# Linear attention: turning the keys with VectorE's block transposes and sixteen small transfers a block instead of TensorE's transposes

## The chip, the cores and the metric

The kernel runs on one core of a Trainium2 chip. The metric is the device time of one execution in microseconds (us), the median of several runs. TensorE is written PE (its matrix products) and PEld (its weight loads), VectorE DVE, ScalarE ACT, GpSimd POOL, and the queue of SyncE, which issues most transfers, SP. SBUF is the on-chip memory of 128 partitions, PSUM the accumulator that TensorE writes.

## The reference, cut to what matters

A two-layer model on a hidden state of 4 x 1024 tokens x 256. The change is in the second layer's attention: linear attention with 16 heads of dimension 128 and a decay for each head. The kernel works with blocks of 128 tokens (the reference with blocks of 32, which gives the same sums):

```
q, k, v = silu(x @ w_qkv)            # per head
for each block of tokens:
    inter = (q * q_decay) @ kv                   # kv: the head's state, 128 x 128
    intra = ((q @ k.T) * diag_decay) @ v
    kv    = block_decay * kv + (k * k_decay).T @ v
    out   = inter + intra
out = rmsnorm(out) * gate; y = out @ w_out
```

The product `(k * k_decay).T @ v` sums over tokens, so TensorE wants the keys with tokens on the partitions. The projections leave them with the head's dimension on the partitions (`kT`), as `q @ k.T` wants them. So each block of keys is turned, 128 x 128 for each of the four sequences.

## The kernel before, in words

The program is a row of phases; the one in question, `linear_attention_phase`, runs from about 1224 to 2630 us. Its engines run their own instruction lists and meet at semaphores. A loop goes over eight pairs of heads; within a pair, sixteen steps are written out, one for each block c of 128 tokens (0 to 7) and each head j of the pair (0, 1). One step works on all four sequences: tiles are 128 partitions x 4 x 128 columns of float32. A state is needed by the next block only, so keys are turned and states made for blocks 0 to 6: fourteen turns in a pair, 112 in all.

TensorE's order within a step i with c < 7 (lines of the profile in brackets):

1. scores S = k q of this step (L1996, eight products),
2. **four transposes of this step's keys** into the PSUM tile KT (L2003),
3. the projections of the next step's queries and keys into PJ (`project_qk`, L1937),
4. output O = v sd (L2018), and, from block 1, O += kv qd (L2021),
5. the state's product KT = kd v (L2026), into the same PSUM tile KT that held the turned keys,
6. the projections of values (L1968) and of the next step's gate (L1937),
7. the output projection (L1981).

For blocks with c = 7 the transposes and the state's product are missing. In blocks with c = 0 item 4 has half its products.

VectorE's order in a step: `sd` = S times the decays (L2101); `kd` = turned keys times their decay, read from KT (L2107); `go` = gate times O (L2116); `kv`, the state, updated from KT (L2121, L2124); `gol`, the low part of go (L2130); the output sum (L2083, two halves). ScalarE makes `qT` (L1867) and `kT` (L1871) of the next step from PJ, then goh, the squares, the values and the gate. `kT` has two buffers, one for each j; KT, kd and O have one.

SP loads the next pair's decays and weights at the beginning of each pair, once the buffers are free (`load_decays` L1807, `load_pair` L1801 to L1803), and does nothing else in this phase.

Of the kernel before, what the change touches and what calls it, by code (L numbers as in the profile page):

```python
# [21 lines left out]
ALU = mybir.AluOpType  # L22
# [3 lines left out]
P = 128  # L26
# [14 lines left out]
def done(step):  # L41

    return step + 1 + CREDIT
# [35 lines left out]
def give_credit(eng, *sems):  # L79
    for s in sems:  # L80
        eng.sem_inc(s, CREDIT)  # L81
# [1653 lines left out]
def linear_attention_phase(nc, X, XH, XL, ident, raw, wo_raw, dec_in, w_qkv, w_gate, w_out, rms_w, decays, kdec, bdec,  # L1735
# [5 lines left out]
    H, DH, BLK = LH, 128, LBLK  # L1741
    NBLK = SEQ // BLK
    HD = H * DH
    B4 = BATCH
    with Phase(nc, "lin") as ph:
# [10 lines left out]
        kT = ph.sb("kT", [P, 2, B4, BLK])  # L1756
# [2 lines left out]
        qd = ph.sb("qd", [P, B4, BLK])  # L1759
        sd = ph.sb("sd", [P, B4, BLK])  # L1760
        kd = ph.sb("kd", [P, B4, DH])
        kv = ph.sb("kv", [P, 2, B4, DH])
        o2 = ph.sb("o2", [P, B4, BLK])
        go = ph.sb("go", [P, B4, BLK])
# [4 lines left out]
        KT = ph.ps("KT", [P, B4, P])  # L1769
# [1 line left out]
        OUT = ph.ps("OUT", [P, 2, 2, D])  # L1771
        VP = ph.ps("VP", [P, 2, 2 * DH])
        (w_in, wo_in, wo_scaled, woh_ready, act_goh, dve_gol, rms_in, dec_loaded, x_in, dec_ready, wh_ready, wl_ready, wo_ready, memsets, sum_set,
         pe_q, pe_k, pe_v, pe_g, pe_s, pe_kt, pe_o, pe_kv, pe_out0, pe_out1, pe_sum,
         act_q, act_k, act_v, act_g, act_sq, pool_qd, pool_sum,
         dve_sd, dve_kd, dve_kv, dve_go, dve_acc0, dve_acc1, mean_ready, root_ready) = ph.sems(
            "w_in wo_in wo_scaled woh_ready act_goh dve_gol rms_in dec_loaded x_in dec_ready wh_ready wl_ready wo_ready memsets sum_set "
            "pe_q pe_k pe_v pe_g pe_s pe_kt pe_o pe_kv pe_out0 pe_out1 pe_sum "
            "act_q act_k act_v act_g act_sq pool_qd pool_sum "
            "dve_sd dve_kd dve_kv dve_go dve_acc0 dve_acc1 mean_ready root_ready")  # L1780
        pe_out = (pe_out0, pe_out1)
        dve_acc = (dve_acc0, dve_acc1)
        xh = XH[:].rearrange("p k (b c l) -> p k b c l", b=B4, c=NBLK)
        xl = XL[:].rearrange("p k (b c l) -> p k b c l", b=B4, c=NBLK)
        acc_v = acc[:].rearrange("p (b c) n -> p b c n", b=B4)
# [4 lines left out]
        HP, TURNS = H // 2, 2 * NBLK  # L1790
        LAST = NBLK - 1
        STATES = 2 * LAST
        block = ph.block()

        @block.sync
        def _(sp):
            sp.dma_start(rms[:], rms_w.rearrange("(h p) -> p h", p=P), allow_slow_non_contiguous=True).then_inc(rms_in, 16)

            def load_pair(g):
                for w in range(3):  # L1800
                    sp.dma_start(raw[:, w], wqkv_v[:, :, bass.ds(g * 2 * DH + w * HD, 2 * DH)]).then_inc(w_in, 16)  # L1801
                sp.dma_start(raw[:, G], wg_v[:, :, bass.ds(g * 2 * DH, 2 * DH)]).then_inc(w_in, 16)
                sp.dma_start(wo_raw[:], w_out[bass.ds(g * 2 * DH, 2 * DH), :].rearrange("(j p) n -> p j n", p=P))\  # L1803
                    .then_inc(wo_in, 16)

            def load_decays(g):
                sp.dma_start(dec_in[:], decays[bass.ds(g * 2, 2)].rearrange("j p w l -> p j w l")).then_inc(dec_loaded, 16)  # L1807

            sp.dma_start(x_first, x_rows[0:RT * P, :].rearrange("(t p) n -> p t n", p=P)).then_inc(x_in, 16)
            sp.sem_inc(w_in, 64)  # L1810
            sp.sem_inc(wo_in, 16)
            sp.sem_inc(dec_loaded, 16)
            with sp.Fori(0, HP - 1) as g:

                sp.wait_ge(dec_ready, g + 1)
                load_decays(g + 1)
                sp.wait_ge(wl_ready, 2 * (g + 1))
                sp.wait_ge(wo_ready, 2 * (g + 1))
                load_pair(g + 1)

            sp.wait_ge(wl_ready, 2 * HP)
            sp.wait_ge(wo_ready, 2 * HP)
            load_pair(0)
            sp.wait_ge(w_in, 64 * (HP + 1))
            sp.wait_ge(wo_in, 16 * (HP + 1))
            sp.wait_ge(x_in, 16)

        @block.gpsimd
        def _(pool):
# [98 lines left out]

        @block.tensor
        def _(pe):  # L1930
            give_credit(pe, pe_q, pe_k, pe_v, pe_g, pe_s, pe_kt, pe_o, pe_kv, pe_out0, pe_out1)

            def project(bank, w, c, j, sem):
                n = 0
# [54 lines left out]
            with pe.Fori(0, HP) as g:  # L1989
                for c, j in itertools.product(range(NBLK), range(2)):  # L1990
                    i = g * TURNS + 2 * c + j

                    pe.wait_ge(act_k, done(i))
                    pe.wait_ge(dve_sd, done(i - 1))
                    for b in range(B4):
                        ins = nc.tensor.matmul(S[:, b, :], kT[:, j, b, :], qT[:, j, b, :], start=True, stop=True)  # L1996
                    ins.then_inc(pe_s, 1)

                    if c < LAST:
                        if (c, j) != (0, 0):  # L2000
                            pe.wait_ge(dve_kv, g * STATES + 2 * c + j)
                        for b in range(B4):
                            ins = nc.tensor.transpose(KT[:, b, :], kT[:, j, b, :], ident[:])  # L2003
                        ins.then_inc(pe_kt, 1)
                        project_qk(i + 1, c + j, 1 - j, g)
                    elif j == 0:
                        project_q(i + 1, c, 1, g)
                        pe.wait_ge(dve_kv, g * STATES + 2 * c - 1)
                    else:
                        output(i - 1, g, 0)  # L2010
                        pe.wait_ge(dve_kv, g * STATES + 2 * c)

                    pe.wait_ge(act_v, done(g * TURNS + 2 * c + 1))
                    pe.wait_ge(dve_sd, done(i))
                    pe.wait_ge(pool_qd, done(i))
                    pe.wait_ge(act_sq, done(i - 1))
                    for b in range(B4):
                        ins = nc.tensor.matmul(O[:, b, :], v[:, c % 2, b, j * DH:(j + 1) * DH], sd[:, b, :],  # L2018
                                               start=True, stop=(c == 0))
                        if c:  # L2020
                            ins = nc.tensor.matmul(O[:, b, :], kv[:, j, b, :], qd[:, b, :], start=False, stop=True)  # L2021
                    ins.then_inc(pe_o, 1)
                    if c < LAST:
                        pe.wait_ge(dve_kd, done(g * STATES + 2 * c + j))
                        for b in range(B4):
                            ins = nc.tensor.matmul(KT[:, b, :], kd[:, b, :], v[:, c % 2, b, j * DH:(j + 1) * DH],  # L2026
                                                   start=True, stop=True)
                        ins.then_inc(pe_kv, 1)
                        project_v(g * TURNS + 2 * (c + 1) + j, c + 1, j, g)
                        project_g(i + 1, c + j, 1 - j)  # L2030
                        output(i, g, j)
                    elif j == 0:

                        project_k(i + 1, c, 1)
                        project_g(i + 1, c, 1)
                    else:

                        project_qk(i + 1, 0, 0, g + 1)
                        project_v(i + 1, 0, 0, g + 1)
                        output(i, g, j)  # L2040
                        project_g(i + 1, 0, 0)
                        project_v(i + 2, 0, 1, g + 1)
# [12 lines left out]
        def _(dve):  # L2055
# [4 lines left out]
            def weights_low(load, part):  # L2060
                dve.wait_ge(wh_ready, 2 * load + part + 1)
                pair = PARTS[part]
                nc.vector.tensor_tensor(WL[:, pair], raw[:, pair], WH[:, pair].bitcast(F32), ALU.subtract)\  # L2063
                    .then_inc(wl_ready, 1)
# [13 lines left out]
            def add_output(i, c):  # L2078
                for half in range(2):
# [2 lines left out]
                    dst = acc_v[:, 2 * half:2 * half + 2, c, :]  # L2082
                    nc.vector.tensor_tensor(dst, OUT[:, half], dst, ALU.add).then_inc(dve_acc[half], 1)  # L2083

            weights_low(0, 0)
            weights_low(0, 1)
            weights_out(0, (slice(0, 1), slice(1, 2)))
            dve.wait_ge(memsets, 2)
            with dve.Fori(0, HP) as g:
                for c, j in itertools.product(range(NBLK), range(2)):  # L2090
# [10 lines left out]
                    nc.vector.tensor_tensor(sd[:], S[:], dec[:, j, 1:2, :].to_broadcast([P, B4, BLK]),  # L2101
                                            ALU.mult).then_inc(dve_sd, 1)
                    if c < LAST:
                        dve.wait_ge(pe_kt, done(g * STATES + 2 * c + j))
                        if (c, j) != (0, 0):
                            dve.wait_ge(pe_kv, done(g * STATES + 2 * c + j - 1))
                        nc.vector.tensor_scalar(kd[:], KT[:], kdec[:, bass.ds(h, 1)], None, ALU.mult)\  # L2107
                            .then_inc(dve_kd, 1)
                    if (c, j) == (LAST, 1):
                        weights_low(g + 1, 0)  # L2110
                        weights_low(g + 1, 1)
# [16 lines left out]
                    dve.wait_ge(act_goh, done(i))  # L2128
                    dve.wait_ge(pe_out1, done(i - 1))
                    nc.vector.tensor_tensor(gol[:], go[:], goh[:].bitcast(F32), ALU.subtract).then_inc(dve_gol, 1)  # L2130
                    if (c, j) != (LAST, 0):
                        add_output(i, c)
                    if (c, j) == (LAST, 1):
# [750 lines left out]
```

## Time and profile before

| what | value |
|---|---|
| median of 3 runs | 2929.03 us (2929.02 to 2929.56) |
| profiled execution, its span | 2929.3 us |
| busy over the span | PE 2694.3 (92%), PEld 2176.9, DVE 1654.2 (56%), ACT 1414.2, POOL 795.0 |
| one pair of heads | 172.9 us from the first S to the next pair's first S |
| one step with blocks 1 to 6 | 10.98 us |

The span is the whole profiled execution, and the profiled execution's time is its span. Busy time counts an engine's instructions and not its waits; a busy TensorE is not one at its peak.

### The profile page before, as it was taken

What the parts mean: (1) busy time and instruction counts of PE and PEld (TensorE: products, weight loads), DVE (VectorE), ACT (ScalarE), POOL (GpSimd) and SP (SyncE); (2) the same over time, 40 slices, a digit from 0 to 9 for tenths busy, and PEclk for the clock granted to TensorE, in tenths of its full rate; (3) what the DMA queues carried; (4) which work ended last, traced back from release to release, by engine and by line L of the source; (5) the groups of instructions that cost most, each with busy time, mean ns of one, the idle gap of its engine ahead of it and who ended that gap; (6) DMA issues with size and microseconds to landing.
All of it is one profiled execution on the core that took longest, in us unless ns stands there. A gap on an engine that the chain in (4) does not pass through costs nothing. (4 is left out here: it accounts for less than half of the span.)

```text
span 2929.3 us, 50261 instructions
## 1 busy us (share of the span) xinstructions
PE 2694.3 (92%) x17642; PEld 2176.9 (74%) x17642; DVE 1654.2 (56%) x3185; ACT 1414.2 (48%) x2605; POOL 795.0 (27%) x803
## 2 busy tenths in 40 slices
PE   7899999979799999599999999999999999995673
PEld 6444444458578888499999999999999999983552
DVE  7688888546588888544444444444444444448321
ACT  6477777756478788533333333333333333336310
POOL 3522222200062222122222222222222222223574
PEclk9799999999999999699999999999999999996666
DMA  8955555030065454300000000000000000004476
GB/s 256 204 100 71 78 75 75 3 99 3 11 240 194 179 189 155 117 1 1 23 1 23 1 1 23 1 23 1 23 1 1 23 1 19 1 1 162 105 165 129
DMA packets 158354, 203.44 MB, mean 69 GB/s; under 512 B 17472, under 2 KB 134880, under 8 KB 149408
## 3 DMA queue, kind: packets, MB, share of 16 engines
q1 hardware_dynamic: 149904, 186.14, 23.8%
q0 software_dynamic: 8256, 14.52, 2.8%
q8 instruction: 145, 2.38, 0.3%
q14 instruction: 49, 0.40, 0.0%
HBM read 154.04 MB, written 50.78 MB: 70 GB/s over the span
## 5 line engine op out<-in xcount | busy, mean ns | idle before, releaser
L1847 POOL TENSOR_TENSOR lin_o2sum<-lin_o2sum,lin_o 128x512 f32<-128x512 f32 x128 | 186.4, 1456 | 995.5 <-ACT lin_o L1890 995.5
L875 DVE TENSOR_REDUCE score_pm<-score_SM 128x1 f32<-128x512 f32 (+3 forms) x608 | 364.5, 657 | 81.6 <-PE score_SM L735 48.8
L829 ACT ACTIVATE score_PR<-score_SE 128x512 f32<-128x512 f32 (+1 forms) x640 | 309.9, 557 | 107.2 <-PE score_SE L763 103.6
L2083 DVE TENSOR_TENSOR C_acc<-lin_OUT,C_acc 128x512 f32<-128x512 f32 x256 | 176.4, 692 | 260.4 <-PE lin_OUT L1981 258.9
L2116 DVE SCALAR_TENSOR_TENSOR lin_go<-lin_gT,lin_O 128x512 f32<-128x512 f32 x128 | 88.1, 689 | 412.6 <-PE lin_O L2021 368.0
L1867 ACT ACTIVATE lin_qT<-lin_PJ 128x512 f32<-128x512 f32 x129 | 77.0, 597 | 426.7 <-PE lin_PJ L1937 419.7
L1937 PE MATMUL lin_PJ<-C_XH,lin_WH 128*128 128x512 f32 x774 | 254.3, 410 | 8.4 <-DVE lin_WL L2063 8.4
L1937 PE MATMUL lin_PJ<-C_XL,lin_WH 128*128 128x512 f32 x774 | 241.6, 393 | 0.0
L1937 PE MATMUL lin_PJ<-C_XH,lin_WL 128*128 128x512 f32 x774 | 241.2, 393 | 0.0
L735 PE MATMUL score_SM<-A_KR,A_QR 96*128 96x512 bf16 (+3 forms) x768 | 229.4, 339 | 12.8 <-DVEq L81 9.6
L763 PE MATMUL score_SE<-A_QR,A_KR 99*128 99x512 bf16 (+3 forms) x768 | 210.6, 330 | 2.0 <-ACT score_PR L829 1.5
L1895 ACT ACTIVATE lin_goh<-lin_go 128x512 fp32r<-128x512 f32 x128 | 81.1, 633 | 243.7 <-DVE lin_go L2116 243.7
L1636 ACT ACTIVATE experts_h<-experts_z 128x512 f32<-128x512 f32 x256 | 161.2, 630 | 71.3 <-DVE experts_z L1541 67.4
L2018 PE MATMUL lin_O<-lin_sd,lin_v 128*128 128x128 f32 x1024 | 190.1, 275 | 2.4 <-POOL lin_qd L1842 2.4
L1541 DVE SCALAR_TENSOR_TENSOR experts_z<-experts_HP,experts_sq 128x512 f32<-128x512 f32 x256 | 174.1, 686 | 17.5 <-PE experts_HP L1673 14.0
L1842 POOL TENSOR_TENSOR lin_qd<-lin_qT,lin_dec 128x512 f32<-128x512 f32 x128 | 166.3, 1299 | 41.0 <-DVE lin_dec L2097 41.0
L2021 PE MATMUL lin_O<-lin_qd,lin_kv 128*128 128x128 f32 x896 | 173.2, 275 | 0.0
L702 POOL TENSOR_SCALAR_AFFINE_SELECT score_PR<-score_PR 128x512 f32<-128x512 f32 x128 | 80.0, 637 | 334.5 <-ACT score_PR L829 334.5
L1937 PEld LDWEIGHTS lin_PJ<-C_XL,lin_WH 128*128 128x128 f32 x774 | 145.9, 189 | 33.4
L1937 PEld LDWEIGHTS lin_PJ<-C_XH,lin_WL 128*128 128x128 f32 x774 | 145.9, 188 | 33.0
L2018 PEld LDWEIGHTS lin_O<-lin_sd,lin_v 128*128 128x128 f32 x1024 | 160.2, 191 | 13.3 <-issue 3.8
L1548 DVE TENSOR_TENSOR experts_hl<-experts_h,experts_hh 128x512 fp32r<-128x512 f32 x192 | 140.7, 733 | 32.2 <-ACT experts_hh L1637 23.2
(355 smaller groups left out, 6574.9 us busy)
## 6 DMA issues: line engine op xcount, KB each, us to landing
experts_sq<-B_roots SPq DMA_DIRECT2D x64, 1024.0 KB, 4.6
A_QR<-q_parts SPq DMA_DIRECT2D x96, 128.0 KB
A_KR<-k_parts SPq DMA_DIRECT2D x96, 128.0 KB
kept_GU<-L_ffn_gate_up_proj SPq DMA_DIRECT2D x48, 192.0 KB
v_rows<-inp_vt SPq DMA_DIRECT2D x32, 256.0 KB, 4.2
A_V<-v_rows SPq DMA_DIRECT2D x16, 512.0 KB
C_w<-L_attn_w_qkv SPq DMA_DIRECT2D x27, 256.0 KB
q_parts<-inp_parts SPq DMA_DIRECT2D x16, 384.0 KB, 3.7
```

What stands on the lines that cost most here:

```text
L735: ins = nc.tensor.matmul(SM[:, count % RING, at:at + nk], QR[0:ROWS_QK, u, h0 + j, t * P:(t + 1) * P], KR[0:ROWS_QK, u, h0 + j, k0:k0 + nk ...
L763: ins = nc.tensor.matmul(SE[:, e % RING, at:at + nq], KR[0:ROWS_ALL, u, h, kt * P:(kt + 1) * P], QR[0:ROWS_ALL, u, h, q:q + nq], start=Tru ...
L829: nc.scalar.activation(PR[:, st % BUFS, h, 0:width], SE[:, e % RING, 0:width], ACT.Exp, scale=SCALE)\
L875: nc.vector.tensor_reduce(pm[:, n % 2, h0:h0 + nh, t, k0 // CHUNK], SM[:, count % RING, 0:nh * nk].rearrange("p (h k) -> p h k", h=nh), AX ...
L1541: nc.vector.scalar_tensor_tensor(z[:, e % 2], HP[:, e % BUFS], 0.0, sq[:, (e // QE) % BUFS, e % QE], ALU.max, ALU.mult).then_inc(dve_z, 1)
L1636: nc.scalar.activation(h[:, e % BUFS], z[:, e % 2], ACT.Square).then_inc(act_h, 1)
L1842: nc.gpsimd.tensor_tensor(qd[:], qT[:, j], dec[:, j, 0:1, :].to_broadcast([P, B4, BLK]), ALU.mult).then_inc(pool_qd, 1)
L1847: nc.gpsimd.tensor_tensor(o2sum[:, c], o2sum[:, c], o2[:], ALU.add).then_inc(pool_sum, 1)
L1937: ins = nc.tensor.matmul(PJ[:, bank], a[:, w, k, j * DH:(j + 1) * DH], x[:, k, :, c, :], start=(n == 0), stop=(n == 3 * KD - 1))
L2018: ins = nc.tensor.matmul(O[:, b, :], v[:, c % 2, b, j * DH:(j + 1) * DH], sd[:, b, :], start=True, stop=(c == 0))
L2021: ins = nc.tensor.matmul(O[:, b, :], kv[:, j, b, :], qd[:, b, :], start=False, stop=True)
L2083: nc.vector.tensor_tensor(dst, OUT[:, half], dst, ALU.add).then_inc(dve_acc[half], 1)
```

## The change

The four transposes on TensorE go. In their place VectorE's `transpose` turns each 32 x 32 square of `kT` where it stands (into `kblk`), and SP issues sixteen SBUF-to-SBUF transfers that bring the squares to their places in `krow`, tokens on the partitions. Each transfer moves 32 partitions x 4 sequences x 32 floats: 128 runs of 128 bytes, 16 KB. VectorE's `kd` is now made from `krow` in SBUF. KT is now the state's product alone, so TensorE's wait for `dve_kv` moves from the transposes to that product.

The turn of step i+1 is issued on VectorE in step i right behind `kd` (for a pair's first turn, behind `gol` of the pair before). SP waits for it and issues its sixteen transfers. `kd` of step i+1 waits for all sixteen. `kblk` and `krow` have two buffers, one for each j. SP's loads of the next pair's decays and weights move from the beginning of a pair to behind the transfers of its last turn (c = 6, j = 1), and the last pair's loads of them take in the decays too.

```
+        QUADS = P // 32
+        def after(c, j):
+            return (c, 1) if j == 0 else ((c + 1) % NBLK, 0)

 # SP
+            def key_rows(g, c, j):
+                sp.wait_ge(dve_kblk, g * STATES + 2 * c + j + 1)
+                for q, d in itertools.product(range(QUADS), range(QUADS)):
+                    tokens, dims = slice(32 * q, 32 * (q + 1)), slice(32 * d, 32 * (d + 1))
+                    sp.dma_start(krow[tokens, j, :, dims], kblk[dims, j, :, tokens]).then_inc(k_in[j], 16)
+            key_rows(0, 0, 0)
+            def head_pair(g, following):
+                for c, j in itertools.product(range(NBLK), range(2)):
+                    c1, j1 = after(c, j)
+                    if (c, j) == (LAST, 1):
+                        key_rows(g + 1, 0, 0)
+                    elif c1 < LAST:
+                        key_rows(g, c1, j1)
+                    elif (c1, j1) == (LAST, 0):
+                        sp.wait_ge(dec_ready, g + 1)
+                        load_decays(following)
+                        sp.wait_ge(wl_ready, 2 * (g + 1))
+                        sp.wait_ge(wo_ready, 2 * (g + 1))
+                        load_pair(following)

 # TensorE
-                        if (c, j) != (0, 0):
-                            pe.wait_ge(dve_kv, g * STATES + 2 * c + j)
-                        for b in range(B4):
-                            ins = nc.tensor.transpose(KT[:, b, :], kT[:, j, b, :], ident[:])
-                        ins.then_inc(pe_kt, 1)
                         project_qk(i + 1, c + j, 1 - j, g)
...
                     if c < LAST:
+                        if (c, j) != (0, 0):
+                            pe.wait_ge(dve_kv, g * STATES + 2 * c + j)
                         pe.wait_ge(dve_kd, done(g * STATES + 2 * c + j))

 # VectorE
+            def key_blocks(i, g, c, j):
+                dve.wait_ge(k_in[j], 16 * QUADS * QUADS * (g * LAST + c + 1))
+                dve.wait_ge(act_k, done(i))
+                nc.vector.transpose(kblk[:, j].rearrange("p b l -> p (b l)"), kT[:, j].rearrange("p b l -> p (b l)"))\
+                    .then_inc(dve_kblk, 1)
...
             weights_out(0, (slice(0, 1), slice(1, 2)))
+            key_blocks(0, 0, 0, 0)
...
-                        dve.wait_ge(pe_kt, done(g * STATES + 2 * c + j))
+                        dve.wait_ge(k_in[j], 16 * QUADS * QUADS * (g * LAST + c + 2))
                         if (c, j) != (0, 0):
                             dve.wait_ge(pe_kv, done(g * STATES + 2 * c + j - 1))
-                        nc.vector.tensor_scalar(kd[:], KT[:], kdec[:, bass.ds(h, 1)], None, ALU.mult)\
+                        nc.vector.tensor_scalar(kd[:], krow[:, j], kdec[:, bass.ds(h, 1)], None, ALU.mult)\
                             .then_inc(dve_kd, 1)
+                    c1, j1 = after(c, j)
+                    if c1 < LAST and (c, j) != (LAST, 1):
+                        key_blocks(i + 1, g, c1, j1)
...
                     nc.vector.tensor_tensor(gol[:], go[:], goh[:].bitcast(F32), ALU.subtract).then_inc(dve_gol, 1)
+                    if (c, j) == (LAST, 1):
+                        key_blocks(i + 1, g + 1, 0, 0)
```

## Rows read from the trace of the kernel before

**Rows 1.** The page, its first line: the whole execution.

```profile
span 2929.3 us, 50261 instructions
```

**Rows 2.** First pair: window, busy PE, PEld, DVE, ACT, POOL; PE's clock, DMA share, GB/s.

```profile
1238.60:1410.50 171.90, 171.60 (x1210) 159.23 (x1208) 77.90 (x116) 58.03 (x98) 42.15 (x31) 1.00 0.03 9
```

**Rows 3.** Timeline of PE over a steady step: start us, us, instruction.

```profile
2006.12 1.05 PE L1996 MATMUL lin_S<-lin_qT,lin_kT 128*128 128x128 f32 x8
2007.01 0.60 PE L2003 MATMUL lin_KT<-ident,lin_kT 128*128 128x128 f32 x4
2007.37 0.71 PE L1937 MATMUL lin_PJ<-C_XH,lin_WH 128*128 128x512 f32 x2
...
2011.99 1.06 PE L2026 MATMUL lin_KT<-lin_v,lin_kd 128*128 128x128 f32 x8
...
2022.97 1.06 PE L2026 MATMUL lin_KT<-lin_v,lin_kd 128*128 128x128 f32 x8
```

**Rows 4.** Timeline of PE, a step with c = 7 (no transposes).

```profile
1390.66 1.05 PE L1996 MATMUL lin_S<-lin_qT,lin_kT 128*128 128x128 f32 x8
1391.47 0.71 PE L1937 MATMUL lin_PJ<-C_XH,lin_WH 128*128 128x512 f32 x2
```

**Rows 5.** Timeline of ACT and DVE in the steady step.

```profile
2010.40 0.60 ACT L1871 ACTIVATE lin_kT<-lin_PJ 128x512 f32<-128x512 f32 x1 [0.68 <-PE lin_PJ L1937]
2012.19 0.69 DVE L2116 SCALAR_TENSOR_TENSOR lin_go<-lin_gT,lin_O 128x512 f32<-128x512 f32 x1 [3.63 <-PE lin_O L2021]
```

**Rows 6.** VectorE on SBUF alone, by tile: ns min/median/max, first and last start us.

```profile
L2097 DVE TENSOR_SCALAR lin_dec<-C_dec x8: 426/426/429, 1236.0 to 2449.5; 128x512 f32<-128x512 f32 x8
L2063 DVE TENSOR_TENSOR lin_WL<-C_w,lin_WH x18: 1210/1222/1758, 1227.4 to 2612.9; 128x1024 fp32r<-128x1024 f32 x18
```

**Rows 7.** Timeline of SP in the first layer's attention: loads issued back to back.

```profile
137.13 0.43 SPq L629 DMA_DIRECT2D A_KR<-k_parts  x1
...
141.35 0.43 SPq L629 DMA_DIRECT2D A_V<-v_rows  x1
```

**Rows 8.** Timeline of SP ahead of the linear attention.

```profile
1189.49 0.47 SPq L213 DMA_DIRECT2D C_dec<-decays  x1
1190.00 0.47 SPq L213 DMA_DIRECT2D x_rows<-X  x1
```

**Rows 9.** Time from issue to landing, tiles rank_w, front_rootT and score_slopes in this order.

```profile
DMA to landing us min/median/max: 1.9/1.9/2.1
...
DMA to landing us min/median/max: 1.6/1.6/1.6
...
DMA to landing us min/median/max: 2.7/2.7/2.7
```

**Rows 10.** Timeline of ACT and SP: a tile's end and the transfer waiting for it.

```profile
697.65 0.59 ACT L1249 ACTIVATE front_rootT<-front_RT 32x512 f32<-32x512 f32 x1 [0.74 <-PE front_RT L1155]
698.26 0.33 SPq L1035 DMA_DIRECT2D B_roots<-front_rootT  x1
```

**Rows 11.** DMA queue over 2713.0 to 2714.2 us: packets of rank_w, MB, engines' share.

```profile
q1 hardware_dynamic: 444, 0.08, 33.6%
```

**Rows 12.** Busy time, clock, DMA share and GB/s while loads queue up.

```profile
105.60:112.00 6.40, 5.79 (x29) 2.40 (x27) 6.05 (x11) 0.00 (x0) 6.29 (x3) 0.77 1.04 135
```

**Rows 13.** Timeline of PE at the second pair's beginning: the states' products.

```profile
1416.60 1.06 PE L2026 MATMUL lin_KT<-lin_v,lin_kd 128*128 128x128 f32 x8
...
1426.70 1.06 PE L2026 MATMUL lin_KT<-lin_v,lin_kd 128*128 128x128 f32 x8
...
1437.68 1.06 PE L2026 MATMUL lin_KT<-lin_v,lin_kd 128*128 128x128 f32 x8
```

**Rows 14.** Timeline of ACT there: the keys of the first two steps.

```profile
1405.10 0.60 ACT L1871 ACTIVATE lin_kT<-lin_PJ 128x512 f32<-128x512 f32 x1 [0.38 <-PE lin_PJ L1937]
...
1415.91 0.60 ACT L1871 ACTIVATE lin_kT<-lin_PJ 128x512 f32<-128x512 f32 x1 [0.77 <-PE lin_PJ L1937]
```

**Rows 15.** The states' products over the phase, by tile.

```profile
L2026 PE MATMUL lin_KT<-lin_v,lin_kd x896: 275/275/275, 1243.6 to 2598.2; 128*128 128x128 f32 x180
```

More of the change, by code:

```diff
@@ L1761, in linear_attention_phase @@
         kd = ph.sb("kd", [P, B4, DH])
+        kblk = ph.sb("kblk", [P, 2, B4, BLK])
+        krow = ph.sb("krow", [P, 2, B4, DH])
         kv = ph.sb("kv", [P, 2, B4, DH])
@@ L1773, in linear_attention_phase @@
         (w_in, wo_in, wo_scaled, woh_ready, act_goh, dve_gol, rms_in, dec_loaded, x_in, dec_ready, wh_ready, wl_ready, wo_ready, memsets, sum_set,
-         pe_q, pe_k, pe_v, pe_g, pe_s, pe_kt, pe_o, pe_kv, pe_out0, pe_out1, pe_sum,
+         pe_q, pe_k, pe_v, pe_g, pe_s, pe_o, pe_kv, pe_out0, pe_out1, pe_sum,
          act_q, act_k, act_v, act_g, act_sq, pool_qd, pool_sum,
@@ L1777, in linear_attention_phase @@
             "w_in wo_in wo_scaled woh_ready act_goh dve_gol rms_in dec_loaded x_in dec_ready wh_ready wl_ready wo_ready memsets sum_set "
-            "pe_q pe_k pe_v pe_g pe_s pe_kt pe_o pe_kv pe_out0 pe_out1 pe_sum "
+            "pe_q pe_k pe_v pe_g pe_s pe_o pe_kv pe_out0 pe_out1 pe_sum "
             "act_q act_k act_v act_g act_sq pool_qd pool_sum "
@@ L1782, in linear_attention_phase @@
         dve_acc = (dve_acc0, dve_acc1)
+        dve_kblk = ph.sem("dve_kblk")
+        k_in = [ph.sem(f"k_in{j}") for j in range(2)]
         xh = XH[:].rearrange("p k (b c l) -> p k b c l", b=B4, c=NBLK)
@@ L1812, in _ @@
             sp.sem_inc(dec_loaded, 16)
-            with sp.Fori(0, HP - 1) as g:
[L1815 to L1823, printed above, removed]
+            for j in range(2):
+                sp.sem_inc(k_in[j], 16 * QUADS * QUADS)
+            def key_rows(g, c, j):
[17 more added lines that the diff above has]
+                        load_pair(following)
+            with sp.Fori(0, HP - 1) as g:
+                head_pair(g, g + 1)
+            head_pair(HP - 1, 0)
             sp.wait_ge(w_in, 64 * (HP + 1))
             sp.wait_ge(wo_in, 16 * (HP + 1))
+            sp.wait_ge(dec_loaded, 16 * (HP + 1))
             sp.wait_ge(x_in, 16)
+            sp.wait_ge(k_in[0], 16 * QUADS * QUADS * (HP * LAST + 2))
+            sp.wait_ge(k_in[1], 16 * QUADS * QUADS * (HP * LAST + 1))
         @block.gpsimd
@@ L1930, in _ @@
         def _(pe):
-            give_credit(pe, pe_q, pe_k, pe_v, pe_g, pe_s, pe_kt, pe_o, pe_kv, pe_out0, pe_out1)
+            give_credit(pe, pe_q, pe_k, pe_v, pe_g, pe_s, pe_o, pe_kv, pe_out0, pe_out1)
             def project(bank, w, c, j, sem):
```

## The prediction

> **What bounds the kernel now.** I read the page first for the span, 2929.3 us [rows 1]; the median of the runs shown is 2929.03, so the sums below, made against the span, hold for the median within 0.3 us. A change counts as one from about 0.2%, 6 us.
>
> Then the busy time over one pair of heads. The reader is to see that TensorE is busy for 171.60 of 171.90 us at the full clock, 1.00, and that no other engine is busy for half of that time [rows 2]. So this stage is TensorE's list from end to end. What is taken out of that list comes off the span, as long as nothing else then arrives late; what is added to VectorE and SP costs nothing, as long as it lands in time.
>
> Then the timeline of TensorE. Two states' products lie 10.98 us apart (2011.99 and 2022.97): that is a steady step [rows 3]. From the scores (2006.12) to the first projection (2007.37) it takes 1.25 us, with the four transposes between [rows 3]. In a step with c = 7, which has no transposes, the same way takes 1391.47 - 1390.66 = 0.81 us [rows 4].
>
> **What the change removes.** 1.25 - 0.81 = 0.44 us of TensorE a turn. The code has 8 pairs x 14 turns = 112, so 49.3 us, down to 2880.0, if nothing is late. The steady step would be 10.98 - 0.44 = 10.54 us.
>
> **What it adds: one chain a turn.** kT finished on ScalarE; VectorE turns the squares; SP issues sixteen transfers; the last lands; VectorE makes kd; TensorE may make the state's product. Terms:
>
> - VectorE's block transpose, T. No row shows one. Rows of other forms: 0.43 us for an operation of 128 x 512 float32 from SBUF to SBUF with one input, 0.69 for one of 128 x 512 with two, 1.22 for 128 x 1024 [rows 5, 6]. I take 0.69, one pass at the pace of most 128 x 512 rows, and keep 0.43 and 1.22 as ends.
> - Issue, p for each transfer. Nine loads in a row take SP (141.35 - 137.13) / 9 = 0.47 us each, 0.43 of it their own [rows 7]. These have few and long runs, ours 128 short ones. Another row has 0.51 [rows 8]. I take 0.47 and 0.51 as the upper end; a lower p wins little, as will be seen. The last transfer is issued 15p = 7.05 us behind the first.
> - Landing, from issue to the semaphore. 1.6, 1.9 and 2.7 us in three quiet places, the first two from SBUF [rows 9]. I take 1.7, ends 1.6 and 2.7.
> - The engines that move the data. 444 packets of 192 bytes took 33.6% of sixteen engines in 1.2 us [rows 11]: 0.336 x 1.2 x 16 / 444 = 14.5 ns each. A turn has 16 x 128 = 2048 runs, 128 for each engine, 1.9 us, spread over 7 us of issue. So they are not the limit.
> - kd: from SBUF 0.43 instead of PSUM, by the 128 x 512 SBUF row [rows 6].
> - Hand-overs. A tile ready at 697.65 + 0.59 = 698.24 had its transfer issued at 698.26 [rows 10]. I take 0.05 for each of four, since none of these rows has a wait on a landing.
>
> From the start of the turn to the end of kd that is L = 0.69 + 0.05 + 7.05 + 1.7 + 0.05 + 0.43 = 9.97 us.
>
> The Trainium skill, "DMA: Bandwidth & Descriptors", section "Anatomy of one DMA", gives about 2.0 us of fixed time for one transfer, near the rows' 1.6 and 1.9; an estimate by that figure has L at 10.27 and the end at 2888 instead of 2885.
>
> **Does L fit?** Two conditions. First, VectorE works in order: the turn of step i+1 stands behind kd of step i, so turns can't follow one another faster than L. 9.97 is under 10.54, by 0.57. Second, kT of the next step is ready at 2010.40 + 0.60 = 2011.00 [rows 5]; with two more hand-overs kd releases TensorE at 2011.00 + 10.07 = 2021.07. The product that wants it comes at 2022.97 - 0.44 = 2022.53 [rows 3]. It fits by 1.46. Behind the turn VectorE has go, which began at 2012.19 [rows 5]; the turn is done at 2011.74, and even with T = 1.22 at 2012.27, so go is held by 0.1 at most.
>
> In blocks with c = 0 it is tighter. The first turn: kT ready at 1405.70 [rows 14], released at 1415.77; wanted at 1416.60 - 0.44 = 1416.16 [rows 13]. No wait. The second: kT at 1415.91 + 0.60 - 0.44 = 1416.07, released at 1426.14; wanted at 1426.70 - 0.88 = 1425.82: TensorE waits 0.32. The third: its turn starts when kd before it ends, 1426.09, and releases at 1436.11; wanted at 1437.68 - 1.32 + 0.32 = 1436.68 [rows 13]. No wait, and from there the chain gains 0.57 a step. So 8 x 0.32 = 2.6 us.
>
> The very first turn has no pair ahead of it. It goes where the copy of the decays began, 1236.0 [rows 6], releases at 1246.0, and is wanted at 1243.6 - 0.44 = 1243.2 [rows 15]: 2.8 us once.
>
> SP's loads of weights move to the end of a pair, behind the sixteen transfers of the last turn. No key transfers are issued then until the next pair's first turn. Six loads of 256 KB at the 135 GB/s of [rows 12] take 11.7 us, and ScalarE wants them in the pair's last step, a steady step and a step with c = 7 later, some 16 us. I cost the move at nothing, with that margin as its cover; without it a pair would wait a few microseconds, 8 x 3 = 24 in all.
>
> Sum: 2929.3 - 49.3 + 2.6 + 2.8 = **2885 us**.
>
> **Where it tips.** With L above 10.37 the second turn too starts when kd before it ends, and the pair's last state is late against before by 2L - 20.90 + 12 (L - 10.98) = 14 L - 152.66. With some 3.5 us for the first turn it breaks even at L = 10.87, 0.9 us above the sum. One term alone at its upper end: p = 0.51 gives L = 10.57 and about 2896; T = 1.22 gives 10.50 and 2888; landing of 2.7 gives 10.97 and 2940. T and p together give L = 11.10: 8 x 2.74 + 4, 2955. All three give 12.10 and about 3070.
>
> **The rivals.**
>
> Forecast: the transfers are covered, 2880 to 2893. For it: SP's row is even and SP has nothing else to do. Chance 0.58.
>
> Partly covered: L between 10.5 and 10.8, so 2893 to 2923. For it: one term is near its upper end. Chance 0.12.
>
> No change, within 6 us: L near 10.87, or TensorE's 0.44 comes back in another wait. Against the latter: in 171.90 us it waits for 0.3 in all, and go has the margin above. Chance 0.05.
>
> Slower by the chain: VectorE can't take the next turn before kd, and L is over 10.9. It decides from p = 0.53 on, if the rest holds. For it: no row has a transfer from SBUF to SBUF or runs of 128 bytes, and no row a block transpose; sixteen times any error of p counts. Against it: three terms must err in the same way, or one by far. At T and p at their ends 2955. Chance 0.22.
>
> Slower by far: transfers don't overlap, and each pays its landing before the next begins. Then L = 16 x 1.7 + 1.2 = 28.4, and each pair loses 14 x 28.4 - 152.66 = 245 us: about 4890. Against it: while loads of 128 KB (0.47 us each in issue) queued up, the engines were busy throughout (share 1.04) and moved 135 GB/s [rows 12]; one at a time with 1.7 us of landing each would be at most 128 KB / 1.7 us = 77 GB/s. Chance 0.03. By the Trainium skill, same page, section "Rules for kernel authors", many small transfers should be made one large, since under 64 KB one pays mostly overhead, and two to disjoint partition halves serialize; this kernel's are of 16 KB and to disjoint quarters, so that page speaks for this rival. The trace agrees only in so far as a small transfer's time is nearly all fixed.
>
> **How the numbers follow.** The time is that of the likeliest case, 2885. Faster 0.58 + 0.12 = 0.70, same 0.05, slower 0.25. The range begins at 2879, just under no wait at all (2880), and goes to 2955, T and p both at their ends: it leaves out the far part of the slower cases, about 0.16, and little below. The likeliest case's own range is 2880 to 2893.
>
> **What the profile after would show.** Right: no L2003; steady states' products 10.54 apart; the PE's wait for kd under 1 us a pair, at its second turn; sixteen issues 0.47 apart; the block transpose at 0.69; kd at 0.43; the last landing 1.7 behind its issue. Wrong: TensorE waits for kd before the states' product in every step, and these lie apart by the chain's length; the term that grew is then read from SP's rows (issue over 0.53), the landing, or the block transpose over 1.2. If the loads of weights are late, ScalarE's L1860 waits for a transfer at each pair's end.

## The result and the profile after

The changed kernel takes 3197.54 us (median of four runs, 3186.80 to 3201.12) against 2929.30 us (2929.02 to 2931.56) for the kernel before: 1.091 times as long, 95% interval 1.0889 to 1.0926. That is 268 us slower, outside the range given, in the case that the prediction called "slower by the chain".

The page of the changed kernel, its first lines and two groups of the costliest instructions (busy us, mean ns of one, then the engine's idle time ahead of them and what ended it):

```profile
span 3195.6 us, 51469 instructions
## 1 busy us (share of the span) xinstructions
PE 2741.8 (86%) x17194; PEld 2198.1 (69%) x17194; DVE 1721.6 (54%) x3298; ACT 1413.9 (44%) x2605; POOL 793.7 (25%) x803
...
L2144 DVE TENSOR_SCALAR lin_kd<-lin_krow,kdec 128x512 f32<-128x512 f32 x112 | 54.4, 486 | 561.1 <-DMA lin_krow<-lin_kblk 561.1
L2055 PE MATMUL lin_KT<-lin_v,lin_kd 128*128 128x128 f32 x896 | 149.2, 317 | 217.9 <-DVE lin_kd L2144 217.9
```

Two waits are new. VectorE stands 561.1 us, once in each of the 112 turns, until the squares have landed. TensorE stands 217.9 us for kd ahead of the state's product, where before it was busy for all but 0.3 us of a pair [rows 2]. The transposes of [rows 3] are gone, as the change says.

The chain of one turn, from the timeline (start us, us, instruction; in brackets the idle time before it and what ended it). The rows of SP's queue, SPq, stand in a fence of their own, as each comes from a narrower stretch and counts the issues in it:

```profile
2000.04 0.48 DVE L2144 TENSOR_SCALAR lin_kd<-lin_krow,kdec 128x512 f32<-128x512 f32 x1 [5.08 <-DMA lin_krow<-lin_kblk]
2000.44 0.70 DVE L2118 STREAM_TRANSPOSE lin_kblk<-lin_kT 128x512 f32<-128x512 f32 x1
2000.58 1.36 PE L2055 MATMUL lin_KT<-lin_v,lin_kd 128*128 128x128 f32 x8 [1.82 <-DVE lin_kd L2144]
...
2011.19 0.60 ACT L1903 ACTIVATE lin_kT<-lin_PJ 128x512 f32<-128x512 f32 x1 [0.68 <-PE lin_PJ L1969]
...
2013.61 0.48 DVE L2144 TENSOR_SCALAR lin_kd<-lin_krow,kdec 128x512 f32<-128x512 f32 x1 [4.46 <-DMA lin_krow<-lin_kblk]
2014.01 0.70 DVE L2118 STREAM_TRANSPOSE lin_kblk<-lin_kT 128x512 f32<-128x512 f32 x1
2014.15 1.16 PE L2055 MATMUL lin_KT<-lin_v,lin_kd 128*128 128x128 f32 x8 [1.21 <-DVE lin_kd L2144]
```

```profile
2001.17 2.17 SPq L1830 DMA_DIRECT2D lin_krow<-lin_kblk  x2
...
2001.80 8.63 SPq L1830 DMA_DIRECT2D lin_krow<-lin_kblk  x12
...
2011.75 0.60 SPq L1830 DMA_DIRECT2D lin_krow<-lin_kblk  x1
```

The next keys are ready at 2011.79 (ScalarE's row), yet their turn begins at 2014.01, 0.40 us behind the start of the kd that holds VectorE. That is the loop: turn at 2000.44; first issue at 2001.17, 0.73 later; sixteenth issue at 2011.75, 10.58 later; kd at 2013.61, 1.86 later; next turn 0.40 later. Together 13.57 us, where TensorE without a wait would take 10.54. The states' products lie just as far apart, 2014.15 - 2000.58 = 13.57. The keys had lain ready for 2.22 us when their turn began; what a kernel would save that issues the turn ahead of kd on VectorE, no run shows.

What each part takes over all turns, by tile (duration of one in ns, smallest, median, largest; start of the first and last):

```profile
L1830 SPq DMA_DIRECT2D lin_krow<-lin_kblk x1808: 585/601/1774, 1235.9 to 2896.9; - x181
L2144 DVE TENSOR_SCALAR lin_kd<-lin_krow,kdec x112: 485/486/489, 1247.7 to 2863.6; 128x512 f32<-128x512 f32 x112
...
DMA to landing us min/median/max: 1.8/1.8/3.4
```

```profile
L2118 DVE STREAM_TRANSPOSE lin_kblk<-lin_kT x113: 702/704/711, 1235.2 to 2886.0; 128x512 f32<-128x512 f32 x113
```

The issue of one transfer takes 0.601 us of SP, and one starts 0.644 behind the other (the median over all neighbours). 585 ns is the fastest of 1808: this is no mean pulled up by a few. SP's issues alone fill 16 x 0.644 = 10.3 of the 10.54 us that a step could have.

In the turn above fifteen spacings at 0.644 would be 9.66, not 10.58. The rest is the second issue: two issues that begin at 2001.17 end 2.17 us later, so the second, begun at 2001.80, took 1.54. In that stretch the DMA view has, beside the squares' packets, one of 16 KB in the queue for instructions (packets, MB, share of the engines):

```profile
q1 hardware_dynamic: 139, 0.02, 7.1%
q8 instruction: 1, 0.02, 5.8%
```

Of the 1808 issues 78 took more than 0.7 us, and in 74 of them one of that queue's 87 packets begins (with one constant shift of 0.6 us between the two records, chosen for the best agreement). The other 13 packets began while SP stood between two turns, so none fell on an issue of the usual length. The long issues also keep to places in the program: the first, second, fifth, seventh, ninth, tenth and twelfth turn of every pair have at least one long issue, the fourth, sixth, eighth, eleventh and fourteenth none in any pair. It remains an agreement in time: no run changed these packets, so that they cause the long issues is not shown.

The shortest distance from a turn to the next of its pair is 12.62 us; the mean over the 8 x 13 distances is 13.27. Of the 0.65 us between the two, 0.54 lie between the first and the sixteenth issue (9.64 at the shortest, 10.18 in the mean) and 0.1 between the sixteenth issue and kd, as some landings took longer, up to 3.4 us.

### The profile page after: what moved, and what is told of

Same layout as the page of the kernel before. It is cut to its first block and busy times, and to the rows that moved or that the text cites. A ratio compares the mean times of both kernels' runs of the same rounds, so it can differ in the third digit from the quotient of the medians.

```text
span 3195.6 us, 51469 instructions
## 1 busy us (share of the span) xinstructions
PE 2741.8 (86%) x17194; PEld 2198.1 (69%) x17194; DVE 1721.6 (54%) x3298; ACT 1413.9 (44%) x2605; POOL 793.7 (25%) x803
## 5 line engine op out<-in xcount | busy, mean ns | idle before, releaser
L1879 POOL TENSOR_TENSOR lin_o2sum<-lin_o2sum,lin_o 128x512 f32<-128x512 f32 x128 | 172.7, 1349 | 1246.3 <-ACT lin_o L1922 1246.3
L2144 DVE TENSOR_SCALAR lin_kd<-lin_krow,kdec 128x512 f32<-128x512 f32 x112 | 54.4, 486 | 561.1 <-DMA lin_krow<-lin_kblk 561.1
L2055 PE MATMUL lin_KT<-lin_v,lin_kd 128*128 128x128 f32 x896 | 149.2, 317 | 217.9 <-DVE lin_kd L2144 217.9
L2055 PEld LDWEIGHTS lin_KT<-lin_v,lin_kd 128*128 128x128 f32 x896 | 125.0, 216 | 239.2 <-DVE lin_kd L2144 239.2
L1969 PE MATMUL lin_PJ<-C_XH,lin_WH 128*128 128x512 f32 x774 | 263.8, 423 | 8.1 <-DVE lin_WL L2092 8.1
L1874 POOL TENSOR_TENSOR lin_qd<-lin_qT,lin_dec 128x512 f32<-128x512 f32 x128 | 179.0, 1398 | 60.0 <-DVE lin_dec L2134 60.0
L1541 DVE SCALAR_TENSOR_TENSOR experts_z<-experts_HP,experts_sq 128x512 f32<-128x512 f32 x256 | 173.9, 685 | 18.1 <-PE experts_HP L1673 16.3
```

Of the source, the lines that this page charges most:

```text
L1541: nc.vector.scalar_tensor_tensor(z[:, e % 2], HP[:, e % BUFS], 0.0, sq[:, (e // QE) % BUFS, e % QE], ALU.max, ALU.mult).then_inc(dve_z, 1)
L1874: nc.gpsimd.tensor_tensor(qd[:], qT[:, j], dec[:, j, 0:1, :].to_broadcast([P, B4, BLK]), ALU.mult).then_inc(pool_qd, 1)
L1879: nc.gpsimd.tensor_tensor(o2sum[:, c], o2sum[:, c], o2[:], ALU.add).then_inc(pool_sum, 1)
L1969: ins = nc.tensor.matmul(PJ[:, bank], a[:, w, k, j * DH:(j + 1) * DH], x[:, k, :, c, :], start=(n == 0), stop=(n == 3 * KD - 1))
```

## The experiments

**A burst of other transfers.** Is it the shape of the squares that makes an issue long? The kernel before was run with nine bursts of sixteen transfers on SP, in the last pair, where SP has nothing to do. Its core:

```
+ src = XH[:, 0, :]      # SBUF;  scr: another SBUF tile;  far: DRAM
+ for q, d in grid: sp.dma_start(scr[q's 32, :, d's 32 floats], src[d's 32, :, q's 32 floats])   # the squares
+ ... the same partitions; one run a partition; one run of 512 bytes; 16 partitions;
+ ... 128 partitions x 4 runs; 128 partitions x 512 bytes; squares to far; squares from far
```

> The kernel before, with nine bursts of sixteen transfers each added on SP in the last pair of heads, when SP has nothing else to do; each burst lands before the next begins, nothing reads what they bring. The forms differ in one thing at a time: the change's squares (32 partitions x 4 runs of 128 bytes, other partitions at the end); the same without changing partitions; one run for each partition instead of four; one run of 512 bytes; 16 partitions instead of 32; 128 partitions with four runs; 128 partitions with one run of 512 bytes; the squares into DRAM; the squares out of DRAM. In the changed kernel the squares took SP 0.60 us each, 0.64 from one to the next, against the 0.47 that the prediction took from other loads. Theory A, the price hangs on SBUF at both ends: all SBUF-to-SBUF forms stay near 0.60 and the two with DRAM fall to 0.36 to 0.47. Theory B, it hangs on the number of runs: one run for each partition falls under 0.50, 128 partitions with four runs rise over 0.8. Theory C, the changed kernel's surroundings make it (VectorE and transfers waiting for each other): here, in a quiet queue, the change's own form falls to 0.47 or under. The time of the whole stays within 6 us of the kernel before in all three.

The tile's rows, in the order squares (L1834), same partitions (L1837), one run (L1840), 512 bytes (L1843), 16 partitions (L1846), 128 partitions with four runs (L1849) and with one of 512 bytes (L1852), out of DRAM (L1858); then, by the DRAM tile, the squares into DRAM (L1855):

```profile
L1834 SPq DMA_DIRECT2D lin_scr<-C_XH x16: 586/601/1142, 2280.8 to 2291.4; - x16
L1837 SPq DMA_DIRECT2D lin_scr<-C_XH x16: 585/601/1556, 2293.3 to 2303.9; - x16
L1840 SPq DMA_DIRECT2D lin_scr<-C_XH x16: 567/590/592, 2305.7 to 2315.2; - x16
L1843 SPq DMA_DIRECT2D lin_scr<-C_XH x16: 507/591/1815, 2316.9 to 2327.6; - x16
L1846 SPq DMA_DIRECT2D lin_scr<-C_XH x16: 594/596/1704, 2329.4 to 2340.1; - x16
L1849 SPq DMA_DIRECT2D lin_scr<-C_XH x16: 639/640/1249, 2341.9 to 2352.8; - x16
L1852 SPq DMA_DIRECT2D lin_scr<-C_XH x16: 488/601/609, 2354.9 to 2364.4; - x16
L1858 SPq DMA_DIRECT2D lin_scr<-probe_far x16: 567/598/1707, 2378.6 to 2389.6; - x16
```

```profile
L1855 SPq DMA_DIRECT2D probe_far<-C_XH x16: 595/600/1347, 2366.3 to 2376.7; - x16
```

The medians are 0.59 to 0.64 us whatever the number of runs, their length, the partitions or the bytes. So many short runs were not what made the issue dear, and neither were the kernel's surroundings: here TensorE's phase was the one of before. But the two bursts with an end in DRAM cost the same, which left it open why [rows 7] have 0.43. The run took 2930.78 us beside 2929.72 for the kernel before, one run each: the bursts cost nothing that shows.

**Fewer squares.** If the length of the chain decides, leaving out transfers should bring the forecast back, and at a count that can be worked out. Eight and twelve of sixteen:

```
- for q, d in itertools.product(range(QUADS), range(QUADS)):
+ SQUARES = [(q, d) ... if (q + d) % 2]     # eight;  with q != d: twelve
+ for q, d in SQUARES:
```

> The changed kernel with eight of the sixteen transfers of a turn left out (the squares with q + d even), krow set to zero once; so half of the turned keys are zeros. Chain theory (a turn can start only behind the kd before it, and its time is 0.40 + 0.73 + (n - 1) x 0.644 + 1.8 + 0.05 us for n transfers, from the trace of the changed kernel: 12.6 for sixteen): 7.5 us for eight, under the 10.54 of TensorE's list; TensorE waits only at the first turn, the steady step is 10.54, the granted clock is back at 1.00 in this phase, and the time is 2882, 2878 to 2890. Rival (the transfers and VectorE's block transposes disturb the other engines, in SBUF or through the clock): half of the disturbance stays, 2950 to 3080.

> The same with four of the sixteen transfers left out (the squares on the diagonal), so a quarter of the turned keys are zeros. Chain theory: 10.06 us a turn, and 10.6 with the half microsecond a turn that transfers lost to single long issues in the changed kernel; that is just at the step of TensorE's list, so a small wait in some steps: 14 x 10.6 - 152.7 = -4.3 us a pair, 2899, between 2885 and 2915. Rival: three quarters of the disturbance, 3040 to 3140.

Eight: 2884.12 us (2880.53 to 2884.91), 0.984 times the kernel before (0.9824 to 0.9854). Twelve: 2905.32 us (2903.03 to 2907.99), 0.992 times (0.9903 to 0.9933). The waits (us in total, times, longest) for eight, and then for twelve:

```profile
DVE lin_kd L2150 <- DMA lin_krow<-lin_kblk: 12.5, 28, 3.6
```

```profile
DVE lin_kd L2150 <- DMA lin_krow<-lin_kblk: 274.6, 112, 6.1
...
PE lin_KT L2059 <- DVE lin_kd L2150: 18.1, 15, 3.7
```

By the parts above the shortest loop is 0.40 + 0.73 + 0.644 (n - 1) + 1.86 us: 7.50 for eight, 10.07 for twelve, 12.65 for sixteen. Eight is far under the 10.54 of TensorE's step; twelve only just, so that its 18.1 us come in fifteen turns; sixteen is over it in every turn. From eight to twelve the kernel loses 21 us, from twelve to sixteen 292. The tip lies between twelve and sixteen, as the prediction's formula has it, and the forecast itself, 2885, is reached once the transfers fit. With eight the steady step was 10.53 us and TensorE's granted clock 1.00 from 1420 to 2560 us, as expected.

**The transposes put back.** TensorE's clock was lower in the changed kernel, 0.923 in the mean, where runs of the kernel before had 0.941 to 0.947. A rival cause was that TensorE loses time by the clock after its waits. Its four transposes came back, with the wait for `dve_kv` ahead of them, their result unread:

```
+ for b in range(B4):
+     nc.tensor.transpose(KT[:, b, :], kT[:, j, b, :], ident[:])
```

> The changed kernel, all sixteen transfers, with TensorE's four transposes put back at their old place, their result not read. Chain theory: TensorE's list has 1.6 to 3 us of waiting a step, the 0.44 us go into it, and the time stays within 8 us of the changed kernel's 3197. Rival (TensorE's list and its clock set the step: what it does more comes on top, or keeps the clock up): 49 us more, 3246, or the half-speed stretches become fewer and it is 3150 or less.

3194.21 us (3191.26 to 3199.09), 1.090 times the kernel before (1.0885 to 1.0918), no other time than without them, at a mean clock of 0.930. By the 0.44 us of [rows 3, 4] TensorE got 112 x 0.44 = 49 us of work more, and the kernel did not grow by them. Its waits show where they went:

```profile
DVE lin_kd L2148 <- DMA lin_krow<-lin_kblk: 575.5, 112, 8.9
...
PE lin_KT L2059 <- DVE lin_kd L2148: 186.0, 96, 6.1
```

TensorE's wait is 217.9 - 186.0 = 32 us shorter, VectorE's about the same. The stretches below are of the changed kernel and then of this one (window; us, busy PE, PEld, DVE, ACT, POOL; PE's granted clock, DMA share, GB/s):

```profile
2001.00:2014.60 13.60, 12.39 (x77) 11.39 (x76) 5.13 (x9) 3.51 (x6) 2.71 (x2) 0.87 0.13 21
2014.60:2028.00 13.40, 10.85 (x77) 9.92 (x76) 5.20 (x10) 3.52 (x6) 2.56 (x2) 1.00 0.13 21
```

```profile
2001.00:2014.60 13.60, 12.22 (x87) 11.27 (x87) 6.11 (x10) 3.51 (x6) 2.56 (x2) 1.00 0.12 19
```

TensorE was granted 0.87 in the first stretch of the one and 1.00 in that of the other, while the whole times agree. TensorE is not what sets the step any more, neither by its work nor by its clock.

**The turn through DRAM.** If issues set the time, fewer of them should win, even over a longer way. VectorE writes the squares so that all that goes to one quarter of partitions lies together (`kd` reads them back in order); one transfer stores the block in DRAM, SP waits for it, and four transfers fetch 32 partitions x 4 runs of 512 bytes each:

```
- sixteen of  sp.dma_start(krow[tokens, j, :, dims], kblk[dims, j, :, tokens])
+ sp.dma_start(far[j]..., kblk[:, j]...).then_inc(k_far[j], 16)
+ sp.wait_ge(k_far[j], 16 * (g * LAST + c + 1))
+ for q in range(QUADS):
+     sp.dma_start(krow[32 * q:32 * (q + 1), j]..., far[j, :, q]...).then_inc(k_in[j], 16)
```

> The changed kernel with five transfers a turn instead of sixteen: the block transpose writes its squares in another order, one transfer of 128 rows of 2 KB puts them into DRAM, and behind its landing four transfers of 32 partitions x 4 runs of 512 bytes bring them back turned. Computes the same. Chain theory, which counts issues and landings: 0.40 + 0.73 + 2.2 (store to landing) + 0.05 + 3 x 0.64 + 2.3 + 0.1 = 7.7 us a turn, under 10.54; the time is 2882, 2878 to 2895, so faster than the kernel before by 1.6%. Rival (bytes moved or a landing in DRAM cost more than issues): the turn is over 10.9 us and the time over 2930.

2882.16 us (2880.26 to 2884.13, five runs): 0.984 times the kernel before (0.9825 to 0.9852), and 10% less than the changed kernel. Its timeline:

```profile
2004.25 0.71 DVE L2123 STREAM_TRANSPOSE lin_kblk<-lin_kT 128x512 f32<-128x512 f32 x1 [2.28 <-ACT lin_kT L1908]
...
2004.99 0.34 SPq L1831 DMA_DIRECT2D far_keys<-lin_kblk  x1
...
2006.98 1.73 SPq L1834 DMA_DIRECT2D lin_krow<-far_keys  x4
```

The way takes 0.74 to the store, 2.0 for its landing and 1.73 for the four issues; with the median landing of 1.9 us behind the fourth, issued at 2008.3, all has landed by 2010.2. VectorE comes to the next `kd` only behind `sd`, at 2011.41 + 0.69 = 2012.10. So a way with two landings in a row is 6 us long, where the way with one landing and sixteen issues was 13. VectorE waits for transfers 6.4 us in the whole phase (10 times), TensorE for kd not at all, and 47.6 of the 49.3 us come home.

The Trainium skill, "DMA: Bandwidth & Descriptors", section "Rules for kernel authors", asks to make many small transfers one large one, as under 64 KB one pays mostly overhead. The trace agrees, and says which overhead: sixteen transfers of 16 KB became one of 256 KB and four of 64, and it was the issue that shrank, not the landing. The same section of the Trainium skill says that two transfers to disjoint halves of the partitions serialize, since both go over the same sixteen engines. Taken as one landing after the other, as the prediction took it for its slowest rival, this is not what the trace shows: the squares' issues stand 0.644 apart and each lands 1.8 behind its own, so up to three are under way at once.

**Where are both ends?** The loads from DRAM in the kernel above took 0.43 us to issue, those of the first probe 0.60. A second set of bursts, in the kernel before, with a weight in DRAM as the source:

```
+ wsrc = w_qkv[0:P, 0:2048]      # DRAM
+ 16 x 4 runs of 512 bytes from wsrc;  16 x 4 runs of 128 bytes from wsrc;  16 x 4 x 512 bytes from SBUF;
+ 16 x one run of 2 KB from SBUF;  16 x 4 x 512 bytes to DRAM;  4 x 128 partitions x 2 KB from wsrc, then from SBUF;
+ 8 x 16 partitions from wsrc;  8 squares, each behind the landing of the one before
```

> The kernel before with bursts of transfers on SP in the last pair of heads, as in the first such kernel, where all nine forms took SP 0.59 to 0.64 us each, the sixteen squares as well as 128 partitions with one run; while four transfers in the kernel that goes through DRAM took 0.43, from 32 partitions x 4 runs of 512 bytes out of DRAM, and loads in the kernel before 0.43 to 0.47. Forms now: DRAM to SBUF with 4 runs of 512 bytes (sixteen), with 4 runs of 128 (sixteen); SBUF to SBUF with 512 (sixteen), with one run of 2048 (sixteen); SBUF to DRAM with 512 (sixteen); 128 partitions of 2048 bytes out of DRAM (four) and from SBUF (four); 16 partitions x 4 runs of 2048 out of DRAM (eight); the squares one at a time, each landed before the next. Theory D, the source decides: all from DRAM 0.43 to 0.47, all from SBUF 0.60. Theory E, the run decides: runs of 512 and more 0.43 to 0.47, runs of 128 0.60, wherever they come from. Theory F, a row of many in flight decides: sixteen of any form 0.60, four 0.43. One at a time, all three expect 0.30 to 0.37.

By the tiles' rows (from the weight L1837, L1840; from SBUF L1843, L1846; squares one at a time L1861; 128 partitions x 2 KB from the weight L1852, from SBUF L1855; 16 partitions from the weight L1858; then, of the DRAM tile, the store):

```profile
L1837 SPq DMA_DIRECT2D lin_scr<-L_attn_w_qkv x16: 358/432/1482, 2281.4 to 2289.7; - x16
L1840 SPq DMA_DIRECT2D lin_scr<-L_attn_w_qkv x16: 312/432/434, 2291.8 to 2298.8; - x16
L1843 SPq DMA_DIRECT2D lin_scr<-C_XH x16: 596/601/1380, 2300.7 to 2311.2; - x16
L1846 SPq DMA_DIRECT2D lin_scr<-C_XH x16: 558/591/1892, 2313.3 to 2324.1; - x16
L1858 SPq DMA_DIRECT2D lin_scr<-L_attn_w_qkv x8: 347/420/430, 2345.3 to 2348.5; - x8
L1861 SPq DMA_DIRECT2D lin_scr<-C_XH x8: 585/585/687, 2354.8 to 2367.9; - x8
L1852 SPq DMA_DIRECT2D lin_scr<-L_attn_w_qkv x4: 357/433/1836, 2335.0 to 2337.8; - x4
L1855 SPq DMA_DIRECT2D lin_scr<-C_XH x4: 523/602/603, 2341.0 to 2342.8; - x4
```

```profile
L1849 SPq DMA_DIRECT2D probe_far<-C_XH x16: 316/445/452, 2326.0 to 2333.2; - x16
```

In this run a pair of the same shape differs by its ends alone: 0.432 from DRAM, 0.601 from SBUF (four runs of 512 bytes), 0.433 against 0.602 (128 partitions x 2 KB). Runs of 128 bytes out of DRAM have 0.432, so the length of the runs is not it. One at a time, each waiting for the landing before, a square still takes 0.585: not a queue that fills up, contrary to what was expected of that burst. What stays open: why the first probe's two bursts with the DRAM scratch had 0.60 too. This set repeats neither of them: its store has runs of 512 bytes where that one had 128, and its loads come from the weight. By the medians both ends in SBUF always had 0.585 to 0.64; an end in DRAM mostly, but not always, had less. So it is not shown that the ends alone decide. The run took 2930.60 us beside 2930.10 for the kernel before.

**Two queues.** If SP's issue is what costs, another engine's queue can take a share. Eleven squares on SP, five on ScalarE's queue behind the gates:

```
+ ON_SP, ON_ACT = SQUARES[:11], SQUARES[11:]
  # ScalarE, behind gates(i + 1, 1 - j)
+ bring(act, ON_ACT, g, *after(c, j))
```

> The changed kernel with all sixteen transfers, eleven of them issued by SP and five by ScalarE's queue, behind the gate of the step. Computes the same. Chain theory with one issuing queue as the bound: SP's part is 0.40 + 0.73 + 10 x 0.644 + 1.8 + 0.05 = 9.4 us a turn, some 9.9 with the long issues, under 10.54; ScalarE has more than 3 us without work behind the gate and its five land in time; 2885, 2879 to 2900. Rival (the queues share what an issue takes, or transfers' landing is the bound): the turn stays over 11 us, 2950 to 3200.

2901.97 us (2900.44 to 2905.64), 0.991 times the kernel before (0.9893 to 0.9926). The direction is as expected, the time just over the range. The squares by issuing queue (ACTq is ScalarE's), and then three of the waits:

```profile
L1806 SPq DMA_DIRECT2D lin_krow<-lin_kblk x1243: 585/601/2430, 1235.2 to 2593.3; - x178
L1806 ACTq DMA_DIRECT2D lin_krow<-lin_kblk x565: 592/622/1856, 1236.5 to 2591.7; - x189
```

```profile
ACT lin_v L1918 <- issue: 28.9, 8, 4.1
...
ACT lin_qT L1906 <- issue: 11.6, 3, 4.2
...
PE lin_KT L2066 <- DVE lin_kd L2155: 9.1, 13, 3.3
```

Both queues pay their 0.60 to 0.62 us, and side by side they hardly slow each other. The chain fits again but for 9.1 us. Of the 17 us over the forecast that does not explain all; ScalarE stands up to 4.2 us ahead of values and queries with nothing that it waits for, eleven times, 28.9 + 11.6 us in all, and in 37.8 of these 40.5 us the trace has its own issues of squares. How much of that reached TensorE was not taken apart.

The Trainium skill, same page, section "Issuing engines are not separate DMA queues", says that a second issuing engine only saves the time of issue, which is usually small beside the transfer. The trace differs on the second half: here the issue of sixteen took 10.3 us and a landing 1.8, and a second queue was worth 296 us.

## Why the prediction was wrong, step by step

**What bounds the kernel** held. Where the transfers fit (eight squares, or through DRAM) 2882 to 2884 us come out against 2885, so the 0.44 us a turn were TensorE's and come off the span.

**The length of the chain** is the step that failed, by one term of it, the issue p. It was put at 0.47, at most 0.51, by the rows of loads from DRAM [rows 7, 8]; between squares it is 0.644 (0.601 their own). Fifteen of them make 9.66 instead of 7.05 us, 2.6 more, where 0.9 were to spare. The sentence that decides said "p = 0.53". I had written down that no row had a transfer from SBUF to SBUF, and then still closed the range of p at a load from DRAM with 0.51. It was not the dearest: loads between the same two tensors, earlier in the same trace, have 0.54 in the median, over the 0.53 that decides (the second line below; the first is of the line of [rows 7], over its whole run):

```profile
L629 SPq DMA_DIRECT2D A_QR<-q_parts x90: 320/426/1475, 104.6 to 494.1; - x90
...
L317 SPq DMA_DIRECT2D A_QR<-q_parts x6: 487/540/1188, 55.0 to 79.3; - x6
```

The short runs that I named beside it are not the price of the squares: the first probe has 0.59 to 0.60 with longer runs as well. Both ends in SBUF is what all the dear forms of the second probe share; the two bursts of the first that had an end in DRAM and 0.60, and the loads just shown, at 0.43 and 0.54 between the same ends, keep that from being proven.

**A part that no term had:** the issues of 0.7 to 1.8 us, of which 68 of the 113 turns have one to three. They make up 0.54 of the 0.65 us between the loop's shortest length, 12.62, and its mean, 13.27; late landings make up the rest. The trace of before had such issues among the loads of [rows 7], up to 1.475 us (the first line above); the nine that the prediction read had none.

**The other terms** held: block transpose 0.70 (0.69), landing 1.8 (1.7), kd 0.49 (0.43, by the row of another operation). The 2.0 us that the prediction sets beside the landing, by the Trainium skill, "DMA: Bandwidth & Descriptors", section "Anatomy of one DMA", are given there for transfers that GpSimd issues; the squares are SP's. Hand-overs were 0.03 from the transpose to SP and 0.02 from the landing to kd (0.05); the next turn starts 0.40 behind kd's start, 0.08 sooner than the 0.43 + 0.05 counted. The engines that move the data were no limit, their share 0.13.

**The mechanism and its formula** held. By its program VectorE takes the next turn behind kd, and TensorE waits in every turn. With the measured 13.27 for L: 14 x 13.27 - 152.66 = 33.1 us a pair, 8 x 33.1 + 3.5 = 268.5 on 2929.3, that is 3197.8; measured 3197.5. That L is measured on the run itself, so this tests the formula and not the forecast. At the loop's shortest, 12.62, it would be 3125; the other 73 are the long issues for the most part, and the late landings. The price given for the rival, 2955, had T at 1.22, well over the 0.70 measured, and p at 0.51, too low; the two errors offset each other in part.

**Slower by far** did not come: transfers overlap, issued 0.644 apart and landing 1.8 behind their issue. **The move of the loads** to a pair's end cost nothing that shows; in the view of the waits nothing on ScalarE waits for a transfer. **TensorE's clock** was on no list; it fell in stretches and cost nothing that shows: with the transposes put back the mean clock was 0.930 for 0.923 and the time the same.

## What to carry to other kernels

Price a chain of small transfers by their issue first, count times spacing, and take that spacing from a transfer with the same two ends: here one from DRAM, at 0.47, stood in for one within SBUF, at 0.644. If a term is multiplied by sixteen and no row has its like, the range must take in the dearest issues that the trace has, and some more, and not stop at one even row of another kind. And fewer, larger transfers can win over a longer way: five issues with two landings took 6 us, sixteen with one landing 13, and the turn through DRAM is the version that beats both kernels.

## What the runs showed of the hardware that was not expected

- Issuing a transfer on SP with both ends in SBUF took 0.585 to 0.64 us, by the median of each form tried, 16 to 128 partitions, one run or four, 128 bytes to 2 KB. With one end in DRAM the bursts of the second probe took 0.42 to 0.45 and two bursts of the first 0.60. On ScalarE's queue the squares took 0.62.
- 78 of 1808 such issues took 0.7 to 1.8 us, and 74 of these have a 16 KB packet of the instruction queue beginning in them; no issue of the usual length has one, by the same shift.
- VectorE's block transpose of 128 x 512 float32 took 0.70 us, as long as its operations with two inputs.
- After a wait of 1.82 us of TensorE ahead of the state's product the projection of the values took 0.63 us for two products, and 0.40 after a wait of 1.21 in the next step; the stretches have a granted clock of 0.87 and 1.00, so the lower of the two levels for a part of the first. These are two steps, and no run shows that the length of the wait decides. One pair of products of each:

```profile
2002.17 0.63 PE L2000 MATMUL lin_VP<-lin_WH,C_XL 128*128 128x256 f32 x2
...
2015.38 0.40 PE L2000 MATMUL lin_VP<-lin_WH,C_XL 128*128 128x256 f32 x2
```
